# Product keys layer: the pairwise sums of all four heads on VectorE, instead of two on ScalarE

## The reference

```python
def _L2_ffn_ref(x, Wq, keys, e_down, e_up):
    H, K, DK = (4, 8, 64)      # heads, kept, width of a key
    E = 2048                   # experts = 16 * 128 in use
    NK = 128                   # keys of each half
    q = (x @ Wq).reshape(b, t, H, 2, DK)
    sim1 = jnp.einsum('bthd,hkd->bthk', q1, keys[:, :, 0, :])
    sim2 = jnp.einsum('bthd,hkd->bthk', q2, keys[:, :, 1, :])
    s1, i1 = jax.lax.top_k(sim1, K)
    s2, i2 = jax.lax.top_k(sim2, K)
    all_scores = (s1[..., :, None] + s2[..., None, :]).reshape(b, t, H, K * K)
    all_indices = (i1[..., :, None] * NK + i2[..., None, :]).reshape(b, t, H, K * K)
    final_scores, pk_idx = jax.lax.top_k(all_scores, K)
    final_indices = jnp.take_along_axis(all_indices, pk_idx, axis=-1)
    hidden = jnp.einsum('btd,bthkd->bthk', x, e_down[final_indices])
    hidden = jax.nn.silu(hidden) * jax.nn.relu(final_scores)
    return jnp.einsum('bthk,bthkd->btd', hidden, e_up[final_indices])

x = _layernorm(x + _L2_ffn_ref(x, ...), axis=-1)
```

## Time and profile before

| | us |
|---|---|
| median of 3 timed runs | 2472.62 |
| lowest and highest | 2469.23, 2482.57 |
| the profiled execution: its own time | 2461.7 |
| its span, first to last instruction | 2460.0 |
| its mean granted TensorE clock | 0.847 of full |
| busy: PE, DVE, ACT, POOL | 1948.6, 1387.2, 897.9, 379.3 |
| `ProductKeys`, first query product to last output | 1427.5 to 1653.9 |

### The profile page before, as it was taken

The page is one execution under the profiler, slowest core; times in us unless marked ns, Lnnn a source line. Parts: engine busy times, 40 slices in busy tenths (PEclk is TensorE's granted clock), DMA queues, the critical chain, the costliest instruction groups (busy, mean ns, idle before and its releaser), DMA issues.

```text
span 2460.0 us, 29350 instructions
## 1 busy us (share of the span) xinstructions
PE 1948.6 (79%) x10453; PEld 1326.8 (54%) x10462; DVE 1387.2 (56%) x2488; ACT 897.9 (37%) x2329; POOL 379.3 (15%) x313
## 2 busy tenths in 40 slices
PE   5655778647546766788888969979999999999895
PEld 3433445314323455566666848865666855556753
DVE  3369957779985825465565128883666144444114
ACT  1445502255322044555555035533554034443000
POOL 2304510015302033332332000000000000000000
PEclk9975577755577989898898989997999999999966
DMA  4000020100101110000001020000001000000000
GB/s 111 7 35 1 0 58 5 49 5 1 44 0 16 23 45 1 20 13 11 11 13 53 1 77 1 1 1 7 11 9 47 1 18 13 11 9 20 35 1 17
DMA packets 25743, 49.19 MB, mean 20 GB/s; under 512 B 6262, under 2 KB 19603, under 8 KB 24092
## 3 DMA queue, kind: packets, MB, share of 16 engines
q1 hardware_dynamic: 25644, 47.85, 6.5%
HBM read 42.20 MB, written 1.05 MB: 18 GB/s over the span
## 4 chain that ended last, share of the span: by engine, by line
PE 60%; DVE 24%; ACT 6%; issue 6%; SPq 2%; DMA 1%; POOL 1%; DVEq 0%; ACTq 0%; POOLq 0%; PEldq 0%
PE banks L1309 8%; PE banks L1278 7%; PE banks L1318 7%; PE banks L1247 7%; DVE big L936 6%; PE banks L1301 4%; DVE big L556 3%; PE banks L1543 2%; PE banks L1953 2%; PE banks L1932 2%; PE banks L463 2%; PE banks L474 2%; ACT big L2059 1%; DVE arena L1365 1%; DVE big L1637 1%
## 5 line engine op out<-in xcount | busy, mean ns | idle before, releaser
L1384 DVE COPY arena<-banks 128x512 f32<-128x512 f32 x196 | 135.6, 692 | 327.2 <-PE banks L1301 323.6
L1278 PE MATMUL banks<-big 128*128 128x256 f32 x784 | 233.6, 410 | 6.0 <-ACT big L1420 4.4
L222 POOL TENSOR_TENSOR ln_rstd<-ln_var_eps,neg_half 128x2 f32<-128x2 f32 x48 | 37.8, 788 | 1283.1 <-DVE ln_var_eps L210 1283.1
L1309 PE MATMUL banks<-arena,big 128*128 128x256 f32 x784 | 226.4, 412 | 6.3 <-DVE arena L1384 6.3
L1441 ACT ACTIVATE arena<-banks,arena 128x256 f32<-128x256 f32 x392 | 193.4, 500 | 61.1 <-DVE arena L1358 43.2
L1459 ACT ACTIVATE big<-banks 128x256 f32 (+1 forms) x196 | 75.3, 384 | 344.8 <-PE banks L1309 344.8
L1247 PE MATMUL banks<-x_feat,arena 128*128 128x512 f32 x392 | 178.0, 597 | 0.0
L1318 PE MATMUL banks<-arena,big 128*128 128x256 f32 x784 | 174.3, 382 | 1.9 <-ACT big L1459 1.9
L1309 PEld LDWEIGHTS banks<-arena,big 128*128 128x128 f32 x784 | 140.0, 196 | 64.4 <-DVE arena L1384 43.3
L1365 DVE TENSOR_SCALAR arena<-arena 128x256 f32<-128x256 f32 x392 | 166.1, 466 | 7.2 <-DVE arena L1363 0.3
L1352 DVE TENSOR_REDUCE arena<-banks 128x2 f32<-128x512 f32 x196 | 134.2, 685 | 61.5 <-PE banks L1278 43.2
(11 more groups left out here) (310 smaller groups left out, 3426.0 us busy)
## 6 DMA issues: line engine op xcount, KB each, us to landing
big<-big SPq DMA_DIRECT2D x32, 64.0 KB, 2.3
arena<-in_L0f_w SPq DMA_DIRECT2D x1, 2048.0 KB, 8.2
arena<-in_L1a_wo SPq DMA_DIRECT2D x1, 2048.0 KB
arena<-in_L1f_gv SPq DMA_DIRECT2D x1, 2048.0 KB
arena<-in_L2a_qk_w SPq DMA_DIRECT2D x1, 2048.0 KB
big<-big SPq DMA_DIRECT2D x64, 32.0 KB
arena<-in_L2x_wo SPq DMA_DIRECT2D x1, 2048.0 KB
arena<-in_L2x_q_w SPq DMA_DIRECT2D x16, 128.0 KB, 2.0
```

What stands on the lines that cost most here:

```text
L1278: last = mm(ps[:, h * SEQ:(h + 1) * SEQ], q[:, b * SEQ + h * P:b * SEQ + (h + 1) * P], k[:, b * SEQ:(b + 1) * SEQ], start=True, stop=not s ...
L1309: last = mm(slot, self.v[:, 2 * b + kc, :], self.probs_t[:, u % 2, kc, :], start=(kc == 0), stop=(kc == 1))
L1384: v.tensor_copy(self.probs_t[:, u % 2].rearrange("p a b -> p (a b)"), B[4 + u % 2][:]).then_inc(self.turn_read, 1)
```

## The change

The tuple `BY_ACT` is empty, and the two buffers of ScalarE's sums are gone. With an empty tuple the list `sums` has two buffers for VectorE instead of one, `vector` makes the sums of all four heads with L2016 and never waits for `summed`, and `scalar` issues no L2059. Per tile VectorE has two more instructions of 128x2048, and ScalarE 32 fewer of 128x128. Everything else is as before.

```diff
@@ -1876,7 +1876,6 @@
         self.sums = [big.take(ROWS, PK_KEYS) for _ in range(1 if self.BY_ACT else 2)]
         self.chosen = [big.take(ROWS, PK_KEYS) for _ in range(2)]
         self.hid = [big.take(ROWS, 2 * P) for _ in range(2)]
-        self.act_sums = [big.take(ROWS, PK_KEYS) for _ in range(2)]
         s = e.sem
@@ -1973,7 +1972,7 @@
-    BY_ACT = (1, 3)
+    BY_ACT = ()
```

## The result

| | kernel before | changed kernel |
|---|---|---|
| median, us (17 runs each) | 2472.28 | 2484.39 |
| lowest to highest | 2457.22 to 2482.69 | 2474.24 to 2500.41 |
| ratio, 95% interval | | 1.0061 [1.0036, 1.0086] |
| two more comparisons of the same pair | | 1.0023 [1.0001, 1.0045], 1.0041 [1.0020, 1.0062] |
| profiled execution: time, span | 2461.7, 2460.0 | 2484.6, 2482.9 |

The changed kernel is slower in each of the three comparisons, by 10 us (0.42%) as the mean of the three ratios; the forecast was +10.3. Nearly all of it is in the layer that the change touches, 9.1 us in this pair of profiles.

A forecast was written before the change was run, and what follows sets the result against it. TensorE bounds the middle tiles; VectorE would become the bound. Tile 0 -4.3, tiles 1 to 7 +0.25, +5.6, +2.6, +4.6 and tail +1.5 sum to +10.3 us, 2482.9 us (+0.42%) on the median; range 2472 to 2496.

The forecast's parts named there:

- The new bound: ProductKeys tiles: VectorE needs 24.83 us a tile with two more sums, TensorE 22.56, so VectorE becomes the bound.
- three meeting points: Within one tile, where VectorE needs TensorE's transposing passes: none late, with 3.3, 4.4 and 1.4 us to spare.
- rival 2: Tiles 1 to 6: engines still wait for each other, 26.5 us a tile, +20 in all, 2493 us; chance 0.10.
- The cost of a sum: VectorE's queue: each added 128x2048 sum takes 2286 ns, 2.31 us of queue; two a tile add 4.62 us.
- rival 3: VectorE's sums fit into its waits, TensorE stays the bound at 22.56 us a tile; about -9, 2464; chance 0.06.
- Tile 0: First tile: the wait for ScalarE goes, TensorE's first transposing pass limits the gain; tile 1 starts 4.3 us earlier.
- Tiles 1 to 7: Later tiles: +0.25 in tile 1, +5.6 in 2 to 5, +2.6 in 6, +4.6 in 7.
- The tail: After tile 7, last pass, mix and output: +1.5 us for a possible clock fall, bounds -0.3 and +5.
- Rival 1: Clock falls in every tile, about 1 us a tile, 6 more: +16, 2489 us; chance 0.15.
- The rule on transposes: Last output: transposes don't engage full clock, so the output starts at half rate and the tail costs +5, not +1.5.
- The saving on ScalarE: ScalarE loses 256 instructions, 76.3 us, but TensorE waits for it by only 0.6 us a time.

The follow-up runs named there:

- kernel 7: Against the kernel before: ScalarE makes no sums and those of heads 1 and 3 are left out, computation incomplete; layer stage 194.4 us, -12.1.
- kernel 3: Against the kernel before: VectorE makes all four sums in tile 0 alone, later tiles unchanged; stage 199.7 us (-6.9), timed ratio 0.9976.
- kernel 4: Against the kernel before: ScalarE makes sums of heads 1 and 3 in tile 0 alone, VectorE all others; stage 225.5 us, +19.0.
- Kernel 10: Against the kernel before: VectorE makes all sums in tiles 0 to 5, ScalarE keeps heads 1 and 3 in tiles 6 and 7; stage 206.5 us, -0.1.
- kernel 2: Against the kernel before: ScalarE keeps only head 1's sums, VectorE makes those of heads 0, 2 and 3; stage 211.8 us, +5.3.
- kernel 8: Against the changed kernel: all sums on VectorE but in a single buffer; stage 219.4 us, 3.8 over the changed kernel.
- kernel 1: Against the kernel before: ScalarE keeps only head 3's sums, VectorE makes the others; 2460.39 us beside 2464.96, ratio 0.9989.
- kernel 5: Against the kernel before: ScalarE makes head 3's sums in tiles 0 to 5, heads 1 and 3 in tiles 6 and 7; 2454.90 us beside 2471.70, 0.9963.
- kernel 6: Against the kernel before: GpSimd instead of ScalarE makes the sums of heads 1 and 3; stage 215.6 us (+9.1), timed ratio 1.0035.

## Why the prediction was right

- **The new bound.** "DVE becomes the bound", at 24.83 us a tile: 24.86 in each of tiles 1 to 6 (tile 7, to its end, 25.1), and no wait of VectorE in them. The layout of one tile held at its three meeting points, so rival 2 (the engines wait for each other) had no part.
- **The cost of a sum** was read from sixteen instructions, 2286 ns; the 32 of now take 2287. That settles rival 3, and kernel 7 shows what it would have taken: at no cost for the added sums TensorE's 22.53 us a tile remain.
- **Tile 0**: 31.2 us expected, 31.30 measured. VectorE's product of head 2 started 23.6 us into the tile, as worked out. It would have been easy to book the whole 17.37 us of the wait as a gain; 8.80 of it turned into a wait for TensorE and two sums filled 4.6. Kernels 3 and 4 bear it out, but show where this number holds: where TensorE sets the pace afterwards, tile 1 gains as well (kernel 3, 2.35 us, or 0.56 beside the second profile of before).
- **Tiles 1 to 7**: +0.29, +5.75, +2.65 and, to the end of tile 7, +4.9 measured, for +0.25, +5.6, +2.6 and +4.6. Kernel 10 gives tiles 6 and 7 back to ScalarE and gets 9.2 us for the 7.3 that they had cost, since tile 6 doesn't wait for a late TensorE as it did before (20.21 for 22.21).
- **The tail** was the term that missed, by 1.7 us. I took +1.5; it was -0.24 in all three profiles of the changed kernel (the last `mix` 2.13 us after the tile for 2.37), its lower end. The clock did fall in tile 7 (0.80 in the mean), as foreseen, but was back at full before the last pass. In tile 6, where it was to fall as well, it stayed at full up to its last 0.4 us (0.99). In kernels 2, 4 and 8 it fell with the last pass, behind gaps of 3.28 to 3.40 us (1.57 in the changed kernel, the row below), and the tail cost 1.4 to 3.1 us more than in the changed kernel, within the bounds. That the sum came out at the measured mean of the timed runs is partly luck: with the tail as measured the prediction's sum is +8.6, with 9.1 in the profile, and the single timed comparisons scatter from +5.7 to +15.1.
- **Rival 1**, the clock in the middle tiles: 1.00 in tiles 0 to 5. It had no part. One of the readings against it was off: of the gaps of 0.78, 0.96 and 2.15 us only the first is in tile 6; the other two end at 1622.75 and 1626.86, in tile 7.
- **The rule on transposes** of the Trainium skill ("TensorE: Matmul & The Clock Gate", Part 4: PE-mode transpose), by which the last output would start at half clock: in the changed kernel nothing but L1941 ran on TensorE between 1659 and 1667, the granted clock rose meanwhile (the windows below), and the output ran at full (7.17 us, the last row). As in the earlier trace rows, the trace disagrees.

```profile
1660.00:1662.00 2.00, 2.00 (x11) 2.00 (x10) 1.96 (x2) 0.00 (x0) 0.00 (x0) 0.50 0.00 0
1662.00:1664.00 2.00, 1.12 (x6) 0.72 (x4) 1.99 (x2) 0.00 (x0) 0.00 (x0) 0.73 0.00 0
1664.00:1666.00 2.00, 1.31 (x12) 1.31 (x13) 0.47 (x3) 0.00 (x0) 0.00 (x0) 1.00 0.00 0
...
1664.69 1.97 PE L1941 MATMUL banks<-ident,big 128*128 128x128 f32 x16 [1.57 <-DVE big L2028]
1667.54 7.17 PE L1952 MATMUL banks<-arena,big 128*128 128x256 f32 x32 [0.88 <-DVE big L1986]
```

- **The saving on ScalarE**, 72 us of busy time, brought nothing by itself; kernels 1, 3 and 5 show that a part of it is worth something, where ScalarE's sums stood in the way: tile 0, and between two Silu. The prediction had this as 0.86 us a tile, and by kernel 7 it is 23.42 - 22.54 = 0.88.

The windows of kernel 5 show both halves at once (tile 1; tiles 2 to 5; tile 6): TensorE is busy throughout until its hidden products end, and then VectorE is back at two sums.

```profile
1479.11:1502.36 23.25, 23.25 (x143) 21.16 (x142) 22.16 (x37) 8.03 (x22) 0.00 (x0) 1.00 0.00 1
1502.36:1592.53 90.17, 90.17 (x546) 82.00 (x545) 88.31 (x145) 34.70 (x96) 0.00 (x0) 1.00 0.00 1
1592.53:1614.15 21.62, 19.26 (x119) 17.05 (x117) 19.78 (x35) 15.24 (x49) 0.00 (x0) 1.00 0.00 0
```

## What to carry to other kernels

Before work is moved between engines, add up each engine's queue for one period and compare the periods: here 20.2 us of VectorE beside 22.6 of TensorE had room for one sum of 2.3 us and not for two, and the engine that was relieved set the pace by 0.9 us only. Then do it for the first and last periods apart, since they have another bound: moved work that hides in the middle stands in the open where the other engine has run out of work. And of a long wait count only what is left when the next releaser is put in: 17.4 us of waiting were worth 4.2 in the tile where they stood.

## What the runs showed of the hardware

- The same pause doesn't give the same clock. In tile 0 of the kernel before TensorE stood still for 2.56 us in one profile and 2.55 in the other; in the first the clock fell to half in the pass behind it (2.55 us for 16 transposes) and stayed there, 0.91 in the mean of the tile; in the second it stayed full (1.97 us, 1.00 in the mean), and tile 1 took 22.79 us for 24.58. The row of the second profile:

```profile
1488.91 1.97 PE L1942 MATMUL banks<-ident,big 128*128 128x128 f32 x16 [2.55 <-DVE big L2019]
```

  So my reading of the earlier trace rows, that a gap of about 2.5 us is where the clock falls, was too firm: it may. Nor does the length of the gap decide in the changed kernel: in its tile 6 the pass behind a gap of 2.63 us ran at full clock, and in its tile 7 the clock fell in the pass behind one of 2.01:

```profile
1634.33 1.97 PE L1941 MATMUL banks<-ident,big 128*128 128x128 f32 x16 [2.63 <-DVE big L2018]
...
1654.85 2.37 PE L1941 MATMUL banks<-ident,big 128*128 128x128 f32 x16 [2.01 <-DVE big L2018]
```

- GpSimd's add of 128x2048 takes 3.61 us beside a VectorE that it holds up and up to 5.53 where it is held up itself; it is no place for work that VectorE's two-input instructions run beside (kernel 6).
